# Ternary weight blocks placed anew among products and queues, and the second FFN weight's blocks stored by set

## The reference, cut to what matters

```python
def _sage_layer(h, edge_src, edge_dst, deg_inv, W_self, W_neigh, b):
    msg = h[edge_src]
    agg = jax.ops.segment_sum(msg, edge_dst, num_segments=h.shape[0])
    mean = agg * deg_inv[:, None]
    return h @ W_self + mean @ W_neigh + b
# gnn: h = relu(_sage_layer(x, ..., W_self0, W_neigh0, b0)); out = _sage_layer(h, ..., W_self1, W_neigh1, b1)
# mix: 16 heads, relu(q) relu(k)^T v / (l * DH), then Wo: linear attention without a softmax
def _quant_weight(w):
    s = jnp.clip(jnp.mean(jnp.abs(w)), EPS, None)
    wq = jnp.clip(jnp.round(w / s), -1.0, 1.0) * s
    return w + jax.lax.stop_gradient(wq - w)
def _quant_act(x):
    scale = 127.0 / jnp.clip(jnp.max(jnp.abs(x), axis=-1, keepdims=True), EPS, None)
    xq = jnp.clip(jnp.round(x * scale), -128.0, 127.0) / scale
    return x + jax.lax.stop_gradient(xq - x)
def _bitlinear(x, w):
    return jnp.einsum('bsi,oi->bso', _quant_act(x), _quant_weight(w))
# ffn: _bitlinear(gelu(_bitlinear(x, w1)), w2)
xn = _layernorm(x, axis=-1)
x = x + gnn(xn, src, dst, ...) + mix(xn, ...)
x = x + ffn(_layernorm(x, axis=-1), w1, w2)
```

## Time and profile before

| | |
|---|---|
| median of 3 runs | 1322.86 us (1322.69 to 1328.53) |
| the profiled execution's own time | 1321.59 us |
| its span | 1319.8 us |
| PE busy | 98% of the span |
| DVE, ACT, POOL busy | 63%, 50%, 7% |
| DMA, mean over the span | 204 GB/s |

### The profile page before, as it was taken

How to read it: one execution, slowest core, us unless ns; L and a number is a source line. 1 busy time by engine, 2 the same in 40 slices (tenths; PEclk the granted TensorE clock), 3 DMA queues, 4 the chain that set the end, 5 groups by cost and what they waited for, 6 DMA issues and landing times.

```text
span 1319.8 us, 18778 instructions
## 1 busy us (share of the span) xinstructions
PE 1296.3 (98%) x6370; PEld 615.3 (47%) x6370; DVE 833.5 (63%) x1467; ACT 661.5 (50%) x905; POOL 90.7 (7%) x91
## 2 busy tenths in 40 slices
PE   9999999999999999999999998998999999999999
PEld 5454445555445444444444443443444444344444
DVE  6854541352677778966983662543546988786774
ACT  7765665355213246523433663854742377464460
POOL 0000000000000002200000111431220100000000
PEclk9999999999999999999999999999999999999999
DMA  8498886864044566616875999998539838723523
GB/s 350 146 280 279 270 289 200 300 216 176 24 167 149 179 209 209 205 49 234 276 252 182 252 262 286 301 283 293 165 115 341 249 96 267 161 61 91 128 53 107
DMA packets 203093, 269.10 MB, mean 204 GB/s; under 512 B 110464, under 2 KB 144000, under 8 KB 199424
## 3 DMA queue, kind: packets, MB, share of 16 engines
q1 hardware_dynamic: 190432, 255.93, 61.2%
q0 software_dynamic: 1440, 5.24, 2.2%
q10 hardware_dynamic: 11136, 6.82, 2.0%
HBM read 184.33 MB, written 57.67 MB: 183 GB/s over the span
## 4 chain that ended last, share of the span: by engine, by line
PE 82%; DMA 6%; DVE 5%; SPq 3%; ACT 2%; issue 1%; ACTq 0%; POOL 0%; DVEq 0%
PE ps L2214 36%; PE ps L2495 12%; PE ps L2345 8%; PE ps L2638 8%; PE ps L2601 7%; PE ps L2536 6%; PE ps L2414 2%; DMA Zb<-blocks_scratch 2%; SPq L650 1%; PE ps L2353 1%; DMA STREAM<-in_w1t 1%; PE ps L2266 1%; DMA HL<-in_w2t 1%; DMA w1q_scratch<-STREAM 1%; PE ps L2248 1%
## 5 line engine op out<-in xcount | busy, mean ns | idle before, releaser
L2214 PE MATMUL ps<-S,XH 128*128 128x512 f16 x1440 | 317.1, 379 | 0.9 <-DVE Zb L1654 0.9
L2214 PEld LDWEIGHTS ps<-S,XH 128*128 128x128 f16 x1440 | 139.9, 98 | 165.9 <-DVE Zb L1654 3.3
L2214 PE MATMUL ps<-S,Zb 128*128 128x512 f16 x480 | 106.4, 379 | 0.0
L2345 PE MATMUL ps<-XH,S 128*128 128x512 f16 (+1 forms) x576 | 102.6, 339 | 0.0
L2214 PE MATMUL ps<-Zb,XH 128*128 128x512 f16 x432 | 94.8, 379 | 0.0
L995 ACT ACTIVATE AT<-ps 128x320 f16<-128x320 f32 x40 | 17.4, 434 | 143.4 <-PE ps L2214 143.3
L1607 DVE TENSOR_SCALAR STREAM<-tables,keys 128x320 f16 x240 | 71.2, 297 | 24.7 <-PE ps L2414 13.2
L2495 PE MATMUL ps<-XH,AT 128*128 128x512 f16 x400 | 86.7, 379 | 0.0
L2495 PE MATMUL ps<-Zb,AT 128*128 128x512 f16 x400 | 86.5, 379 | 0.0
L2345 PEld LDWEIGHTS ps<-XH,S 128*128 128x128 f16 x576 | 56.1, 98 | 47.0 <-issue 2.3
L2214 PEld LDWEIGHTS ps<-S,Zb 128*128 128x128 f16 x480 | 47.0, 98 | 54.4 <-issue 0.6
(11 more groups left out here) (315 smaller groups left out, 1988.8 us busy)
## 6 DMA issues: line engine op xcount, KB each, us to landing
STREAM<-in_w_all SPq DMA_DIRECT2D x48, 512.0 KB, 5.1
STREAM<-in_w1t SPq DMA_DIRECT2D x46, 512.0 KB, 5.2
STREAM<-in_w2t SPq DMA_DIRECT2D x28, 512.0 KB, 5.3
XIN<-in_x SPq DMA_DIRECT2D x20, 512.0 KB, 5.1
Zb<-in_w1t SPq DMA_DIRECT2D x14, 512.0 KB, 7.6
blocks_scratch<-S SPq DMA_DIRECT2D x4, 1792.0 KB, 8.5
blocks_scratch<-STREAM SPq DMA_DIRECT2D x4, 1792.0 KB, 8.6
S<-blocks_scratch SPq DMA_DIRECT2D x7, 1024.0 KB, 10.1
```

What stands on the lines that cost most here:

```text
L2214: last = mm(acc[:, n * BANK:(n + 1) * BANK], left(l, kc), right(kc, r)[:, n * BANK:(n + 1) * BANK], start=(kc == 0 and i == 0), stop=(kc = ...
L2345: last = mm(ps[:, 3 * j * BANK + a:3 * j * BANK + b], Wq_s[:, kc, l, mc], XH[:, r, kc, a:b], start=(kc == 0 and l == 0 and r == 0), stop=( ...
```

## The change

- The ten pairs of stage 1 have 0, 1, 3, 3, 0, 2, 2, 2, 3, 2 blocks in place of 1, 2, 3, 3, 1, 1, 2, 2, 2, 2, 18 in place of 19. The rotation of the three raw buffers starts one place further on, SP sends for blocks 12 and 13 ahead of B11, and the order of rounds and copies in pairs 0 and 1 changes.
- The six other loads of Z1's blocks stand between single stores: the first before block 17's store, five behind it.
- Block 29 moves to the x1 stage, behind row tile 0. Blocks 30 and 31 stay behind tiles 1 and 3. Block 31's raw rows are loaded behind the transpose of tile 3, where they were loaded ahead of the stage. The stores of blocks 29, 30 and 31 are given out behind the transposes of tiles 3, 4 and 6, those of 30 and 31 stood behind those of tiles 2 and 4. DVE's second operation for these three is done by POOL (`all_blocks`).
- `w2q_scratch` is laid out (k s n) in place of (s k n): for each partition, a block's eight sets lie side by side. A store writes 4 KB per partition in a piece, a load of one set reads 16 pieces of 512 B per partition.
- B22's load goes out behind the transpose of tile 9, and the loads of x1 tiles 0 and 1 go out earlier. DVE does x1 of tile 9 inside `x2_scaled(8)`.

```diff
@@ -64,7 +64,7 @@
-LAST_QUADS = 30
+LAST_QUADS = 29
@@ -218,7 +218,7 @@
                 return i % 2
-            return 2 if i <= EDGE_QUADS else 2 + (i - EDGE_QUADS - 1) % 3
+            return 2 if i <= EDGE_QUADS else 2 + (i - EDGE_QUADS) % 3
@@ -251,7 +251,7 @@
-        w2q_parts = w2q_d.rearrange("p (s k n) -> p s k n", s=8, k=HC // 2)
+        w2q_parts = w2q_d.rearrange("p (k s n) -> p k s n", s=8, k=HC // 2)
@@ -330,9 +330,9 @@
-        ST_COUNTS = (1, 2, 3, 3, 1, 1, 2, 2, 2, 2)
+        ST_COUNTS = (0, 1, 3, 3, 0, 2, 2, 2, 3, 2)
...
-        X1_QUADS = {1: 30, 3: 31}
+        X1_QUADS = {0: 29, 1: 30, 3: 31}
@@ -478,9 +478,9 @@
+                if i == EDGE_QUADS + 1:
+                    sp.wait_ge(S("h_turned1"), 64 * PAIRS)
...
-                    sp.wait_ge(S("h_turned1"), 64 * PAIRS)
-                if i == EDGE_QUADS + 3:
@@ -498,7 +498,7 @@
                 else:
-                    to = w2q_parts[:, :, i - W1_QUADS, :]
+                    to = w2q_parts[:, i - W1_QUADS, :, :]
                 sp.wait_ge(S("made_last"), 2 * i + 2)
@@ -593,27 +593,32 @@
-            block_load(sp, 1, "B11")
...
-            quad_load(EDGE_QUADS + 3)
-            quad_store(EDGE_QUADS)
...
-            def st_quads(i):
...
-                for n in ST_QUADS[i]:
-                    if n + 3 < LAST_QUADS:
-                        quad_load(n + 3)
-                    quad_store(n)
...
-            for i in range(1, PAIRS - 1):
-                st_quads(i)
-            for name, product in zip(LOAD_ORDER[1:], ("P1", "P2", "P6", "P7", "P5", "P3")):
-                sp.wait_ge(S("st_ps"), st_done(PAIRS - 1, product))
-                block_load(sp, 1, name)
-            for i in range(PAIRS - 1, 2 * PAIRS):
-                st_quads(i)
+            block_load(sp, 1, "B11")
...
+            def st_quad(n):
...
+                if n + 3 < LAST_QUADS:
+                    quad_load(n + 3)
+                quad_store(n)
...
+            def z1_block(n):
...
+                sp.wait_ge(S("st_ps"), st_done(PAIRS - 1, ("P1", "P2", "P6", "P7", "P5", "P3")[n]))
+                block_load(sp, 1, LOAD_ORDER[1 + n])
...
+            last_s1 = ST_QUADS[PAIRS][0] - 1
+            for n in range(EDGE_QUADS, last_s1):
+                st_quad(n)
+            z1_block(0)
+            quad_store(last_s1)
+            for n in range(1, 6):
+                z1_block(n)
+            quad_load(last_s1 + 3)
+            for n in range(last_s1 + 1, LAST_QUADS):
+                st_quad(n)
@@ -625,10 +630,10 @@
-            for n in range(LAST_QUADS, N_QUADS):
-                quad_load(n)
+            for n in range(2):
+                quad_load(LAST_QUADS + n)
...
-                sp.wait_ge(S(f"made_out{b}"), 16 * LAST_QUADS // 2)
+                sp.wait_ge(S(f"made_out{b}"), 16 * ((LAST_QUADS + 1 - b) // 2))
@@ -654,12 +659,11 @@
-                if t - 1 in X1_QUADS:
-                    quad_store(X1_QUADS[t - 1])
-                if t == 6:
-                    for b in range(2):
-                        sp.wait_ge(S(f"made_out{b}"), 16 * N_QUADS // 2)
-                    sp.dma_start(w2_in_S0, w2q_d[:, 12 * D:16 * D]).then_inc(S("B22_in"), 16)
+                if t - 3 in X1_QUADS:
+                    i = X1_QUADS[t - 3]
+                    if i + 2 < N_QUADS:
+                        quad_load(i + 2)
+                    quad_store(i)
@@ -671,33 +675,36 @@
-                sp.dma_start(W2[name].rearrange("p k n -> p (k n)").bitcast(F16),
-                             w2q_d[:, 4 * D * part:4 * D * (part + 1)]).then_inc(S(f"{name}_in"), 16)
+                sp.dma_start(W2[name].rearrange("p k n -> p (k n)").bitcast(F16).rearrange("p (k n) -> p k n", k=HC // 2),
+                             w2q_parts[:, :, part, :]).then_inc(S(f"{name}_in"), 16)
...
+            def x1_load(t):
+                sp.dma_start(x1_in[:, t % 2, :], rows(x1_d, t)).then_inc(S(f"rows_in{t % 2}"), 16)
...
+            sp.wait_ge(S("out0"), 16 * 4)
+            x1_load(0)
...
+            for b in range(2):
+                sp.wait_ge(S(f"made_out{b}"), 16 * N_QUADS // 2)
...
-            sp.dma_start(w2_in_AT, w2q_d[:, 0:4 * D]).then_inc(S("B11_in"), 16)
-            for name, part in (("B21", 2), ("T3", 6), ("T2", 5)):
+            for name, part in (("B11", 0), ("B21", 2), ("T3", 6), ("T2", 5)):
...
+            sp.wait_ge(S("out1"), 16 * 4)
+            x1_load(1)
...
+            w2_load("B22", 3)
...
-            def x1_load(t):
-                sp.dma_start(x1_in[:, t % 2, :], rows(x1_d, t)).then_inc(S(f"rows_in{t % 2}"), 16)
...
-            for t in range(2):
-                x1_load(t)
@@ -777,8 +784,18 @@
-            for i in range(ST_QUADS[PAIRS][0], N_QUADS):
+            def all_blocks(i):
...
+                made = blocks_made(i)
+                pool.wait_ge(S("made"), 2 * i + 1)
+                nc.gpsimd.tensor_tensor(made[:, 4:8:2, :], made[:, 1:4:2, :], made[:, 0:2, :], ALU.subtract,
+                                        saturate=False).then_inc(S("made"), 1)
...
+            for i in range(ST_QUADS[PAIRS][0], LAST_QUADS):
+                last_blocks(i)
+            for i in range(LAST_QUADS, N_QUADS):
+                all_blocks(i)
@@ -1138,7 +1155,7 @@
-                cuts = {0: (0, 0, 0, 0, 2, 4), 1: (0, 0, 0, 0, 4, 8)}.get(i, (2, 4, 5, 6, 10, 12))
+                cuts = {1: (2, 2, 2, 2, 4, 4)}.get(i, (2, 4, 5, 6, 10, 12))
@@ -1693,14 +1710,18 @@
-            def quad(i):
+            def quad(i, both=True):
...
                 wait(dve, f"made_out{i % 2}", 16 * (i // 2))
+                if i > LAST_QUADS:
+                    dve.wait_ge(S("made"), 2 * i)
                 dve.wait_ge(S("rounded"), 4 * i + 4)
...
                                 saturate=False).then_inc(S("made"), 1)
+                if not both:
+                    return
                 dve.wait_ge(S("made"), 2 * i + 1)
@@ -1913,7 +1934,8 @@
                     z1_lo_rest(i - 1)
-                quad(quads[0])
+                for n in quads[:1]:
+                    quad(n)
                 if i >= PAIRS:
@@ -1948,6 +1970,10 @@
+            def x1_stats(t):
...
+                j = t % 2
@@ -1955,12 +1981,17 @@
-            def x2_scaled(t):
+            def x1_rows(t):
+                x1_add(t)
+                x1_stats(t)
+
+            def x2_scaled(t, after_max=lambda: None):
                 dve.wait_ge(S("ln_std"), NT + t + 1)
...
                 link(V.tensor_reduce(col("y_max"), x2n, AXX, ALU.max, apply_absolute_value=True))
+                after_max()
                 link(V.tensor_scalar(col("y_clip"), col("y_max"), EPS_Q, None, ALU.max))
@@ -1993,7 +2024,7 @@
                 if t - 1 in X1_QUADS:
-                    quad(X1_QUADS[t - 1])
+                    quad(X1_QUADS[t - 1], both=False)
                 if t == 3:
@@ -2172,8 +2203,8 @@
-            x2_scaled(8)
-            x1_rows(9)
+            x2_scaled(8, lambda: x1_add(9))
+            x1_stats(9)
```

More of the change, by code:

```diff
@@ L1940, in _, with x1_add @@
             z1_lo_rest(2 * PAIRS - 1)
-            def x1_rows(t):
+            def x1_add(t):
                 j = t % 2
```

## The result

The changed kernel takes 1335.25 us (median of 5 runs, 1334.91 to 1337.58) against 1322.69 before (5 runs): ratio 1.0095, 95% interval 1.0079 to 1.011. It is slower by 12.6 us, where 4 were forecast and 1334 was the upper end. Its profiled execution has a span of 1333.1 us, 13.3 more than the one before.

What follows compares the result with a forecast made beforehand. PE, busy 98% of the span, was taken as the bound, losing 17.9 us in the middle stage. Terms -16.2 + 15.2 + 1.6 + 4.5 = +5.1 gave 1327 us, range 1316 to 1334.

Steps and rivals of the forecast that it cites:

- part 1: Middle stage of ten pairs: blocks spread anew and Z1 loads between single stores remove PE's waits, gain 16.2 us.
- named gains: Middle stage: PE waits removed, 6.4 us in pair 0, 2.2 in pair 1, 0.25 in pair 4, 7.3 in pair 5.
- I take 16.2: Middle stage: gain taken as 16.2 us, with ends 9 (one of two places waits anew) and 17.
- what hid the moved rounds: Pair 8: ACT gets 18.6 us of work in an 18.1 us pair; waits around it take up the excess.
- Rival D: Middle stage: busy DMA makes block 16's rows late, pair 3 waits; gain 9 instead of 16.2, 1334 us; chance 0.09.
- Part 2: x1 stage and FFN start: block 31's late load and store cost 15.2 us, plus 1.6 for PE's slow start.
- tile 4's deviation: x1 stage: tile 4's standard deviation comes at 1041.2 instead of 1033.39, 7.8 us later, behind block 31's rounds on ACT.
- the 5.4: x1 stage's end: landing time in us of block 31's store, before ACT's first FFN copy.
- The wait at edge sum 7: x1 stage: PE waits 1.8 us for tile 5's x1, which is swallowed by the next step.
- That wins nothing: x1 stage: giving DVE's second operation (1.2 us each) to POOL wins nothing, since PE did not wait there before.
- Part 3: Second FFN product: new weight layout makes loads gather 512 B runs at 294 GB/s; third sum's products 4.5 us later.
- The copy behind y_round: FFN, x1 of tile 9 moved: copy 0.9 us later, one product 0.6 earlier, net 0, give or take 1.

Runs made afterwards that it cites:

- Experiment 4: Changed kernel with POOL's two accumulating stores of pair 0 held until all transposes of h have landed: 1328.86 us, ratio 1.0062 to the kernel before.
- `old_layout`: Changed kernel with the second weight's scratch laid out (s k n) as before, places of loads and stores kept: 1331.17 us, ratio 1.0055 to the kernel before.
- experiment 8: Changed kernel with block 31's load and store early, POOL's pair 0 stores held, old layout (1307.3 us); DVE does its second operation on blocks 29 to 31 again: 1309.26 us.
- `before_late31`: Kernel before with block 31's rows sent for behind tile 3's transpose, its store behind tile 6's, B22's load behind tile 7's: 1343.49 us, ratio 1.0148.
- experiment 3: Changed kernel with B11's load moved behind the raw rows of blocks 14 and 15 and the stores of 11 and 12: 1336.27 us, ratio 1.0088 to the kernel before.

## Why the prediction was wrong

**The step that failed is the sum of part 1.** Its named gains were all there: 5.96 of 6.4 in pair 0, 2.19 of 2.2 in pair 1, 7.52 of 7.5 in pairs 4 and 5. But "I take 16.2" held that only ACT's room could spoil them. The stage gave 7.1, since pair 2 lost 7.09 and the start of pair 0 lost 1.47. I had asked what hid the moved rounds, not what a pair 0 without waits sets going: POOL's stores go out 2 us earlier, SP's last transposes of h went out 2.2 later, and the two meet. By the code, the changed order of buffers made it count, since blocks 12 and 13 now both wait for these transposes, and B11 and block 14 behind them; before, B11 and block 12 went out without waiting. I saw those lines in the diff and gave them no price. Experiment 4 shows that the stores delay the transposes and that this delay cost 5.0 of the 7.1 that pair 2 lost; that the old order of buffers would have borne it was not run. Rival D had the size (9, 1334) and the wrong place, block 16's rows in pair 3.

The 0.95 ahead of pair 0 and the 1.47 at its start are not shown to come from the change. In the experiments' kernels with the changed order the first product of pair 0 starts at 783.7 to 785.9, and P6 waits 0.41 to 1.18 us behind it (9.63 in `old_layout`, below). In the 1.47, what differed is how long ACT took to give out its four loads, after

```profile
785.15 3.76 ACTq L355 DMA_DIRECT2D Zb<-blocks_scratch  x4
```

and before

```profile
784.20 2.29 ACTq L355 DMA_DIRECT2D Zb<-blocks_scratch  x4
```

**Part 2** was forecast at 15.2 and 1.6 and measured 15.07 and 2.02, but two of its terms were off and cancelled. Counted from the first edge sum, tile 4's deviation came 9.0 later (7.8 forecast) and the transpose of tile 6 8.1 later (6.1), while the copy followed the store's issue after 3.3 us, not 5.4. The long runs are only 0.7 of that, which I had put nowhere in part 2: with short runs at the same place (`old_layout`) it followed after 4.0. The rest seems to be the place, since I had taken the 5.4 from block 31's store at 1045.26. The wait at edge sum 7 was 2.83, not 1.8, and was swallowed as said. With the slow products behind it (40 matmuls in 10.49 us, where 40 x 0.216 is 8.6) it comes out of the same 15.07, so PE stood 10.21 at the FFN's start and not 12 to 13. "That wins nothing" of DVE's second operation held nearly, for a reason that I did not have: POOL slows DVE, and 0.3 us per block are left. Undone in experiment 8 it cost 1.07 at the start of the FFN; undone in the changed kernel alone it was not run.

**Part 3** was forecast at 4.5 net and measured 2.33. The rate was right. With only gathers of 512 B under way the DMA engines moved 293 GB/s, with long runs 412 (stretches as in the earlier trace rows, after and before):

```profile
1120.00:1124.00 4.00, 4.00 (x20) 1.73 (x20) 1.11 (x2) 3.26 (x6) 0.00 (x0) 1.00 1.17 293
```

```profile
1109.00:1113.00 4.00, 4.00 (x20) 1.81 (x19) 1.08 (x2) 3.11 (x6) 0.00 (x0) 1.00 1.00 412
```

The span around it was mis-sized: from the first of the six loads to the landing of the transpose of tile 9 I had 29.9 us, measured was 27.9 (1114.89 to 1142.8) against 23.0 before. These 2 us are the difference between 4.5 and 2.33. And the picture was wrong: I had the transpose go out early and land after 26 us, much as in the kernel before, where it took 19.3. It went out 20 us after the first load, since SP was held by the gathers, and landed 8.0 later. The copy behind y_round that came 0.9 later and the product 0.6 earlier are both there and stay at zero.

By the Trainium skill, DMA: Bandwidth & Descriptors, Specifications, 512 B runs should reach line rate and the layout cost nothing. The runs speak against it for this gather: 293 GB/s where long runs had 412, and 3.2 to 4.8 us in three pairs of kernels.

Three slips are in my sums: the losses named make 17.8, not 17.9, the wait at edge sum 7 is 1.7, not 1.8, and 5.1 on the median shown, 1322.86, is 1328, not 1327. None matters here. With the terms as measured the sum is 0.95 - 7.11 + 15.07 + 2.02 + 0.04 + 2.33 = 13.3, the whole difference of the spans.

What stays open: the middle stage has a second way to lose. In the profiled executions of `old_layout` and `before_late31` pair 0 stood 9.63 and 12.18 us. ACT's row in `before_late31`:

```profile
785.24 2.34 ACTq L355 DMA_DIRECT2D Zb<-blocks_scratch  x4
...
800.27 0.63 ACT L1103 ACTIVATE HL<-TMP 128x512 f16<-128x512 f32 x1 [11.59 <-DMA S<-SPLIT]
```

There the transposes ahead of these four loads of 1 MB went out at 783.00 (781.95 in `old_layout`), where before and after it was 780.5. In `old_layout` POOL's stores came so late (816.60) that the last transposes landed after 4.0 us and pair 2 did not wait, which fits the account of pair 2. What makes them 1.5 to 2.5 us late in some executions, and whether ACT's loads are what delays them, no run told apart. Whether B11's place has a price of its own in an execution like the changed kernel's is open too, as experiment 3 did not come to it.

## What to carry to other kernels

Taking a wait away releases what stood behind it: list the transfers that will now start earlier, on every queue, and look which transpose or load they will meet, and who is waiting for it. A buffer that is sent for behind a semaphore of transposes inherits all their delays. And where a stage starts with a wait for "all stores", the last store's place in the queue, and that of the load that feeds it, have a price: here block 31's load and store, each moved one or two places forward, gave 8.3 and 8.4 us back, and both together 14.8.

## What the runs showed of the hardware

- The last two transposes of h, given out together, landed (median) after 4.0 us where the first of POOL's accumulating stores of 512 KB went out 4.8 us or more behind them, and after 7.7 to 13.2 in the five kernels where it went out within 0.7 us of them.
- Gathers of 1 MB in 512 B runs hold the engine that issues them: 9.92 us for three, against 1.68 with 8 KB runs. While they ran, the DMA engines moved 293 GB/s, against 412 with the long runs.
- A float32 tensor_scalar of 128x1024 on DVE took 0.81 us alone, 1.61 beside a 1.09 us and 2.52 beside a 2.00 us float8 operation on POOL.
- After PE had stood 10.21 us, the next products of four matmuls started 1.68, 1.71, 1.21 and 0.87 us apart: the granted clock was at 1.2 GHz for the first ones and then at 2.4, for a cost of 2.0 us.
